# Third half row by DMA in row blocks 29 to 31 of a two-layer graph kernel on one Trainium2 core

## What is computed

```python
deg = clip(adj.sum(axis=1), 1.0); dis = deg ** -0.5
diffusion = (dis[:, None] * adj * dis[None, :]) @ x - x
sim = x @ x.T / (norms[:, None] * norms[None, :])
attn = softmax(beta * sim * adj, axis=1)
x = layernorm(x + diffusion + sigmoid(alpha) * (attn @ x - x))
x = layernorm(x + relu(adj @ (x @ weights)))
```

## Time and profile before

| | us |
|---|---|
| median of 3 runs (653.23 to 655.1) | 654.17 |
| the profiled execution | 653.43 |
| its span, first to last instruction | 651.6 |
| PE busy | 637.5 (98%) |
| DVE busy | 516.1 (79%) |
| ACT busy | 413.7 (63%) |
| POOL busy | 236.9 (36%) |

### The profile page before, as it was taken

The page is one execution under the profiler, slowest core; times in us unless marked ns, Lnnn a source line. Parts: engine busy times, 40 slices in busy tenths (PEclk is TensorE's granted clock), DMA queues, the critical chain, the costliest instruction groups (busy, mean ns, idle before and its releaser), DMA issues.

```text
span 651.6 us, 16130 instructions
## 1 busy us (share of the span) xinstructions
PE 637.5 (98%) x5095; PEld 464.9 (71%) x5095; DVE 516.1 (79%) x1564; ACT 413.7 (63%) x774; POOL 236.9 (36%) x249
## 2 busy tenths in 40 slices
PE   8889999999999999999999999999999999999996
PEld 7457777777777777777777777888888864444465
DVE  5989999999999999999999998868777763334453
ACT  7999999999999999999999998712211110000000
POOL 5999544544544544544644646400000000000000
PEclk9999999999999999999999999999999999999999
DMA  7879999999999999999999996500000000000001
GB/s 280 315 158 260 295 236 247 294 248 246 298 244 246 299 243 241 296 251 248 303 234 254 293 249 105 101 2 2 0 0 0 0 1 1 16 17 18 16 32 33
DMA packets 167100, 107.89 MB, mean 166 GB/s; under 512 B 146464, under 2 KB 150688, under 8 KB 167072
## 3 DMA queue, kind: packets, MB, share of 16 engines
q1 hardware_dynamic: 167072, 107.57, 62.7%
HBM read 69.27 MB, written 2.10 MB: 110 GB/s over the span
## 4 chain that ended last, share of the span: by engine, by line
PE 90%; DVE 3%; ACT 2%; DMA 2%; issue 1%; POOL 1%; SPq 0%; DVEq 0%; ACTq 0%; POOLq 0%
PE ps_s L1023 23%; PE ps_s L1227 17%; PE ps_e L1199 15%; PE ps_acc L1060 8%; PE ps_e L1034 8%; PE ps_e L1060 8%; PE ps_acc L1063 4%; PE ps_e L1063 4%; DMA x_keep<-in_x 1%; DMA eTx<-e_parts 1%; DVE scores L723 1%; ACT scores L537 1%; PE ps_s L1076 1%; PE ps_acc L1211 1%; PE ps_at L1076 1%
## 5 line engine op out<-in xcount | busy, mean ns | idle before, releaser
L1023 PE MATMUL ps_s<-xn_parts,xn_signed 128*128 128x512 f16 x756 | 203.3, 379 | 2.9 <-DVE cmax L723 2.9
L723 DVE CUSTOM_DVE_ANT_1 scores<-ps_s,adj_bytes 128x512 f32<-128x512 f32 x252 | 171.6, 683 | 21.4 <-PE ps_s L1023 14.6
L537 ACT ACTIVATE scores<-scores,col 128x1024 f32<-128x1024 f32 x128 | 157.4, 1232 | 1.2 <-DVE col L734 0.9
L496 ACT ACTIVATE adj_bytes<-land 128x1024 uint8<-128x1024 f32 x128 | 133.5, 1047 | 0.6 <-POOL packed L354 0.6
L362 POOL TENSOR_SCALAR e_parts<-scores 128x1024 f16<-128x1024 f32 x64 | 68.5, 1070 | 153.3 <-ACT scores L537 149.9
L1199 PE MATMUL ps_e<-y_parts,stage 128*128 128x256 f16 x896 | 98.0, 273 | 0.0
L1023 PEld LDWEIGHTS ps_s<-xn_parts,xn_signed 128*128 128x128 f16 x756 | 68.6, 98 | 38.4 <-DVE cmax L723 2.5
L1199 PEld LDWEIGHTS ps_e<-y_parts,stage 128*128 128x128 fp8e4 x896 | 87.7, 98 | 10.1
L544 ACT ACTIVATE eT_parts<-ps_e 128x512 f16<-128x512 f32 x126 | 74.8, 595 | 24.4 <-PE ps_e L1034 23.4
L744 DVE SCALAR_TENSOR_TENSOR e_parts<-scores,e_parts 128x1024 f16<-128x1024 f32 x64 | 88.2, 1380 | 0.4 <-POOL e_parts L362 0.4
L738 DVE SCALAR_TENSOR_TENSOR eT_parts<-ps_e,eT_parts 128x512 f16<-128x512 f32 x126 | 86.0, 683 | 1.8 <-ACT eT_parts L544 1.8
(11 more groups left out here) (139 smaller groups left out, 974.2 us busy)
## 6 DMA issues: line engine op xcount, KB each, us to landing
land<-in_adj SPq DMA_DIRECT2D x128, 512.0 KB, 5.6
x_keep<-in_x SPq DMA_DIRECT2D x4, 512.0 KB, 5.3
out<-u SPq DMA_DIRECT2D x7, 256.0 KB, 2.1
eTx<-e_parts SPq DMA_TRANSPOSE x64, 4.3
packT<-packed SPq DMA_TRANSPOSE x16, 6.7
out<-u SPq DMA_DIRECT2D x2, 128.0 KB, 1.7
scores<-in_L_gnn_weights SPq DMA_DIRECT2D x1, 64.0 KB, 2.7
col<-in_L_gnn_beta SPq DMA_DIRECT2D x1, 0.5 KB, 7.2
```

The source lines that it names most:

```text
L496: nc.scalar.activation(adj_bytes[:, q, i * CH:(i + 1) * CH], land[:, q, i, :], ACT.Copy, scale=float(BYTE_TOP[q] >> i), accum_out=deg[:, i ...
L537: nc.scalar.activation(piece, piece, ACT.Exp, bias=neg_max[q], scale=abs_beta, accum_out=csum[:, q, i:i + 1]).then_inc(exp_done, 1)
L723: nc.vector.tensor_tensor_reduce(scores[:, q, o:o + BANK].rearrange("p (k q) -> p k q", k=K), score_bank(h, r == 0 if start else False).re ...
L1023: ins = nc.tensor.matmul(score_bank(h, start), xn_signed[:, q, part, :], xn_parts[:, other, o:o + BANK], start=(part == 0 and other == 0), ...
```

## The change

Blocks 29 and 30 get what block 31 had: their columns 1024 to 2047 go by POOL, DVE and a transposing DMA, no longer over PE. For that the last round of the loop, block 29, is taken out of it on all engines and written by hand. There is one buffer `third`, used three times, and three buffers `thirdT`. POOL's `third_high(m)` waits for the transpose of the block before (`third_turned`), as it writes the same buffer. `late_turn_e`, `late_e_high` and `late_e_low` are the old steps for b = 0 and 1. In the tail, `late_turn_e(2, ...)` stands ahead of `late_attend(6)` and (7), and the order of a few `sums` is changed. The cut diff (SP, POOL, ACT, DVE, PE, in this order):

```diff
+    SIX_ATTEND = (0, 4, 1, 5, 6, 7, 2, 3)
+    LATE_ATTEND = (0, 1, 4, 5, 6, 7, 2, 3)
     LAST_ATTEND = (0, 1, 4, 5, 6, 7, 2, 3)
-    LATE_ATTEND = (0, 4, 5, 1, 2, 6, 7, 3)
+    SIX = 29
...
+            def turn_third(m):
+                sp.wait_ge(third_lo, m + 1)
+                sp.dma_start_transpose(thirdT[m], third.rearrange("p a j -> p (a j)")).wait_op(
+                    x_loaded[0], 16, "sem-ge").then_inc(third_turned, 16)
             turn_ex(R - 3, 1, 1)
+            turn_third(0)
             turn_ex(R - 2, 0, 0)
             turn_ex(R - 2, 0, 1)
             turn_adj(R // 2 - 1, 1)
+            turn_third(1)
             turn_ex(R - 1, 1, 0)
             turn_ex(R - 1, 1, 1)
-            sp.wait_ge(third_lo, 1)
...
+            turn_third(2)
...
+            def third_high(m):
+                pool.wait_ge(exp_done, (SIX + m) * C + C)
+                if m == 0:
+                    pool.wait_ge(cast_done, (R - 1) * C)
+                else:
+                    pool.wait_ge(third_turned, 16 * m)
+                nc.gpsimd.tensor_scalar(third[:, 0, :], scores[:, (SIX + m) % 2, CH:2 * CH], E_SCALE, 1.0,
+                                        ALU.mult, ALU.mult).wait_op(sign_done, 1, "sem-ge").then_inc(third_hi, 1)
...
             pack(R - 2, 0, R // 2 - 1, 1)
+            third_high(0)
...
             ex_high(R - 2, 0, 1)
+            third_high(1)
             pack(R - 1, 1, R // 2 - 1, 1)
...
+            mask(R - 1, 1, 0)
+            third_low(0)
+            total_step(SIX, 1, 1)
+            mask(R - 1, 1, 1)
+            ex_low(R - 2, 0, 0)
+            attn_add(R - 4, 0)
+            mask(R - 1, 1, 2, third_row=True)
+            total_step(SIX, 1, 2)
+            mask(R - 1, 1, 3, third_row=True)
             mask(R - 1, 1, 4)
-            e_low(R - 2, 0)
+            late_e_low(1, 0)
             ex_low(R - 2, 0, 1)
+            third_low(1)
             mask(R - 1, 1, 5)
+            late_e_low(1, 1)
             mask(R - 1, 1, 6)
             degrees()
             mask(R - 1, 1, 7)
             row_max(R - 1, 1)
...
+            late_turn_e(1, 0)
+            cosines(R - 1, 1, 4)
+            late_turn_e(1, 1)
+            cosines(R - 1, 1, 5)
+            six_attend(5)
+            cosines(R - 1, 1, 6)
+            six_attend(6)
+            six_attend(7)
+            cosines(R - 1, 1, 7)
+            for k in range(6):
+                late_attend(k)
+            late_turn_e(2, 0, LAST_EXP)
+            late_turn_e(2, 1, LAST_EXP)
+            late_attend(6)
+            late_attend(7)
             first_sums(0)
             last_attend(0)
             last_attend(1)
```

More of the change, by code:

```diff
@@ L577, in _, with late_e_high @@
             row(1, 1, order=range(H))
-            with act.Fori(2, R - 3, 2) as r:
+            with act.Fori(2, R - 5, 2) as r:
                 row(r, 0)
                 row(r + 1, 1)
+            row(R - 4, 0)
+            def late_e_high(m, b, order):
+                act.wait_ge(e_turned, SIX * TB + (2 * m + b + 1))
+                act.wait_ge(attn_part, (SIX - 1 + m) * H + (order.index(b) + 1))
+                nc.scalar.activation(eT_parts[:, b, 0, :], ps_e[:, b, :], ACT.Copy, scale=E_SCALE).then_inc(e_hi, 1)
+            for h in range(H):
+                if h in (0, 2):
+                    late_e_high(0, h // 2, ATTEND_ORDER)
+                if h < C:
+                    cast(R - 1, 1, h)
+                else:
+                    exps(R - 2, 0, EXP_ORDER[h - C])
             def y_high(q):
@@ L711, in _, with mask @@
             xnt_low(5)
-            def mask(r, q, h, start=False):
+            def mask(r, q, h, start=False, third_row=False):
                 dve.wait_ge(s_done, r * H + (h + 1))
-                if not start and h < TB:
+                if third_row:
+                    dve.wait_ge(third_lo, 1)
+                elif not start and h < TB:
                     dve.wait_ge(e_turned, r * TB + (h + 1 - 2 * TB))
@@ L878, in _ @@
             row_max(R - 1, 1)
-            e_low(R - 2, 1)
             total_step(R - 2, 0, 0)
             total_step(R - 2, 0, 1)
-            e_low(R - 2, 2)
-            y_low(0)
-            e_low(R - 2, 3)
             attn_add(R - 3, 1)
             total_step(R - 2, 0, 2)
-            e_low(R - 1, 0)
-            e_low(R - 1, 1)
+            y_low(0)
+            late_e_low(2, 0)
+            late_e_low(2, 1)
             y_low(1)
@@ L1036, in turn_e, with attend @@
                 ins.then_inc(e_turned, 1)
-            def attend(r, q, k, start=False, early=False, order=ATTEND_ORDER, last=False):
+            def attend(r, q, k, start=False, early=False, order=ATTEND_ORDER, six=None):
                 b = order[k]
-                if last and b in (2, 3):
-                    pe.wait_ge(third_turned, 16)
+                if six is not None and b < 2:
+                    pe.wait_ge(e_lo, SIX * TB + (2 * six + b + 1))
+                elif six is not None and b < TB:
+                    pe.wait_ge(third_turned, 16 * six + 16)
                 elif b < TB:
@@ L1053, in attend @@
                     t, slot = TH * b + SLOT[n], TH * (b % 2) + n
-                    if last and b in (2, 3):
-                        hi, lo = (thirdT[:, a * TC + slot, :] for a in range(2))
+                    if six is not None and b in (2, 3):
+                        hi, lo = (thirdT[six][:, a * TC + slot, :] for a in range(2))
                     elif b < TB:
@@ L1173, in first_sums @@
                     sums(r, i)
-            turn_e(R - 1, 1, 0, order=LAST_EXP)
-            turn_e(R - 1, 1, 1, order=LAST_EXP)
+            for h in range(H):
+                if h in (0, 2):
+                    late_turn_e(0, h // 2)
+                if h < C:
+                    cosines(R - 2, 0, h + C)
+                else:
+                    cosines(R - 1, 1, h - C)
+                if h >= LAG:
+                    six_attend(h - LAG)
+                else:
+                    attend(R - 4, 0, h + H - LAG)
+            late_turn_e(1, 0)
[13 more added lines that the diff above has]
+            late_attend(7)
             first_sums(0)
```

88 lines of the change are left out of this document (45 added, 43 removed).

## The result

| | before | after |
|---|---|---|
| median, us (lowest to highest) | 654.17 (653.23 to 655.1) | 658.93 (657.53 to 659.15) |
| the profiled execution | 653.43 | 658.93 |
| its span | 651.6 | 657.1 |
| PE busy | 637.5 | 637.5 |
| POOL busy | 236.9 | 241.1 |

The ratio is 1.0065, with an interval of 1.0054 to 1.0077: slower, by 4.3 us. It is taken over all executions and isn't the quotient of the two medians, which lie 4.8 us apart. A second measurement, with twelve executions in place of five, gave 1.0043 (1.0026 to 1.0059), which is 2.8 us. The forecast was +2.5, and 654.3 to 658.6 its range: the first median, 658.93, lies 0.3 above that range, 654.17 times the ratio, 658.4, inside it.

A forecast was written before the change was run, and what follows sets the result against it. PE, 98% busy, bounds the kernel, with the POOL and DVE chain to `y_low(2)` close behind. `y_rows` 2.6 us later shifts `whole_row` about +2.5: 654.17 + 2.5 = 656.7 us, range 654.3 to 658.6.

The forecast's parts named there:

- steps 1 to 5: Main case, block 29 to `whole_row`: later POOL and DVE work delays PE; +1.7 to +3.5 us, chance 0.57 together with (d).
- rival (c): POOL wins the hand-over against DVE's `ex_low`, so `y_rows` starts near 407.5: +4.3 us, 658.5; chance 0.15.
- the chain behind `y_rows`: POOL and DVE operations from `y_rows` to the end of `y_low(2)`: 14.55 us without gaps; if shorter, the prediction is wrong.
- Step 1: `third_high(0)` on POOL holds up block 29's `ex_low` on DVE, 0.7 us late; block 31's first mask goes at about 392.7.
- Step 2: `third_low(0)` and block 30's first `ex_high` and `ex_low` delay the mask of piece 2; `cosines(31, 4)` starts at 398.0, against 397.68.
- The race between POOL and DVE: Block 30: POOL's second `ex_high` and DVE's `ex_low` both ready; DVE was forecast to go first, `ex_low` ending at 396.65.
- Step 3: `third_high(1)` waits for the first transpose, `third_low(1)` follows; `degrees` at 405.0 against 402.39, `cosines(31, 7)` waits until 403.8.
- Step 4: `y_rows` begins 2.6 us later, at 405.7; `y_low(2)` ends at 420.2, so `first_sums(2)` and `whole_row` shift about +2.5 us.
- Step 5: `turn_third(1)`, behind `turn_adj` on SP, lands at 411.5; `late_attend(6)` waits 2.2 us: +1.6 alone, hidden beside step 4.
- (b): Faster: PE's queue alone decides, 1.76 and most of 1.1 us go, 651.3 to 652.4; chance 0.08.
- (d): The third half row's transpose lands late, 5.6 us instead of 4.6: 420.4 and +2.6; chance 0.57 shared with steps 1 to 5.
- (a): POOL and DVE operations overlap more cheaply, `y_rows` at 403.8: +0.5 to +1 us, 654.7 to 655.2; chance 0.2.

## Why the forecast was right in direction and short in size

The case, slower by steps 1 to 5, came about, and the sign with it. The first median lies 2.2 us above the forecast, the second measurement 0.3 above it. By its time alone the first measurement, +4.3, would belong to rival (c), whose mechanism didn't occur. Of the prediction's own signs of being wrong one came true: the chain behind `y_rows` is shorter than 14.55 us. `whole_row` came at 434.0, not at 433.0. By its steps (after's times less 1.93):

- **Step 1** held loosely. `third_high(0)` ran at 387.7 (388 forecast), but `ex_low` beside it was not held up: at 390.70 of after's own time it took 1.22. DVE lost its time one `ex_low` earlier instead, at 387.21, which took 1.75 beside `pack`. `third_low(0)` came at 393.0 (393.3 forecast).
- **Step 2** gave the right time by another way. The race between POOL and DVE didn't take place: POOL's second `ex_high` waited 0.62 for a DMA still reading its buffer. `cosines(31, 4)` started at 397.7 (398.0).
- **Step 3** held: `cosines(31, 7)` 403.4 (403.8), its wait 1.18 (1.4). `third_high(1)` began at 399.0 (399.15), and `pack` had one addition between two operations of DVE, as forecast.
- **Step 4** was too dear. `degrees` came at 404.5, not 405.0, and `y_rows` at 405.2, 2.1 us later than before and not 2.6, and the chain behind it took 13.8 us (407.14 to 420.93), not 14.55. Between `y_rows` and `y_low(2)` lie two `ex_high`, `y_low(1)`, two `ex_low` and the third half row's high part, by my prices 6.57 us together. Before, they took 6.73 (409.77 to 416.50), with a pause of 0.2 ahead of `y_low(1)`; after, 6.07 (413.73 to 419.80). There each waited for the one before it, and one that waits is through a little sooner than its full length: `ex_high` at 415.24 was held by `y_low(1)` to about 415.85 and ended at 416.83, 0.98 later instead of 1.05; `y_low(1)`, held to 414.85, ended 1.00 later instead of 1.14. The floor of step 4 is +1.4, as the run with `first_sums(0)` in front shows, not +2.5.
- **Step 5 is the step that failed.** Its landing was right, 411.7 for 411.5, though by luck in part: the transpose was issued 0.5 earlier than forecast and took 5.4 us instead of 4.6. So the wait was about right too, 2.63 for 2.2. But the forecast then added 1.32 + 2.64 + 1.32 + 2.64 of matmuls at the lengths of the earlier trace rows, which are lengths at full clock. After 2.6 us of idleness they took 1.63 more. So PE came to `first_sums(2)` at 421.3, not at 419.4, and behind a `y_low(2)` that was through at 419.0. "It hides beside step 4" was wrong: step 5 set the end, by 2.1 us. The term that the forecast left out is the clock, 1.63 us; with the seven matmuls in the wait, which kept it up, the same step measured +1.9 for the forecast +1.6. That the second measurement lies so near to the forecast is partly luck. The later of the two steps sets the time; with step 4 at its +1.4 the forecast would have been step 5's +1.6, and the 1.1 too much in step 4 stood in for part of the missing clock.
- Of the rivals, (b) needed `y_rows` at 401.4 and got 405.2; the run without block 30's part shows that it would not have come even then. (c) did not occur. (d) named the right wait, with 420.4 for 421.3, and lacked only the clock. (a) priced the sum of the overlaps, 0.5 to 1 us, and the floor of +1.4 lies between it and the forecast.

The Trainium skill's 115 ns stand in another section than the prediction names (SBUF — State Buffer, A bandwidth-pool intuition that's wrong (but worth ruling out)), and there they were measured on a DMA whose descriptors GpSimd had to write beside a copy of DVE. For the operations of POOL and DVE here the same rows answer them: the chain came out 0.75 shorter than by the row's price, and no row has room for an addition at each hand-over.

## What to carry to other kernels

A wait put on a matmul engine that otherwise never idles has to be priced with the clock behind it: here 2.5 and 2.6 us of waiting cost 1.6 us more in the executions whose traces show the drop. Whatever is put early into the queue of an engine that issues in order, or into a buffer that is used again, delays everything behind it in that queue: follow each new step through POOL, SP and the buffer up to the first consumer, and put work that doesn't need it in front of that consumer, which here took 2.1 of the 3.5 us off the tail. And before taking work off the busiest engine, look how far behind it the next one is; here it was 0.6 us, with a third bound at the same place, and a change that frees 1.8 us had nowhere to put it.

## What I had not expected of the hardware

- **The clock of TensorE falls after a single wait of a few us, in some executions.** It was granted 0.50 behind waits of 2.53 us (at once), 2.63 (after 1.3 us of full-speed work) and 5.15, and kept its full level in the profiled executions with waits of 2.16, 1.83 and 1.71. Behind 2.15 us, in the run with two buffers, it was granted 0.50 too, from 416 to 418, and the first 16 matmuls of `first_sums(0)` took 3.09 instead of 1.91, in an execution that had waited 2.02 some 19 us earlier. So the length of the wait alone doesn't decide: 2.15 lost the clock and 2.16 kept it. Behind the waits of 2.53 and 2.63 us the drop cost 1.6 us each. Matmuls of the identity put into the wait kept it up. The Trainium skill (TensorE: Matmul & The Clock Gate, What's actually happening) describes a gate that passes half the pulses when the array has not been busy of late, and says that its observation runs freely and isn't started anew with a kernel; that one kernel shows the drop in some executions only, and at different distances from the wait, agrees.
- **The same transpose lands after quite different times**: the three of the third half row took 4.5, 5.4 and 6.6 us in one execution, with transposes of `e_parts` and of `packed` in flight beside them. The page's line on them (tiles, engine and operation, count, median to landing):

```profile
land<-land SPq DMA_TRANSPOSE x3, 5.4
```
